# An attention block with a mixture layer on one core: maxima of two PSUM banks in one VectorE operation, a new order of the units, and fewer filler products

## What is computed

```
Xn = layernorm(x) * ln_g + ln_b
Q, K, V = Xn @ Wq + bq, Xn @ Wk + bk, Xn @ Wv + bv      # split in 16 heads
A = softmax(causal(Q K^T / sqrt(16)))
x = layernorm(x + (A V) @ Wo + bo)
```

```
h = relu(x @ W1 + b1);  alpha = softmax(h @ W2 + b2)
x = layernorm(x + sum_k alpha_k * (x @ V_k^T) @ U_k^T)
```

## Time and profile before

| | us |
|---|---|
| median of 3 runs | 436.98 (436.42 to 437.85) |
| profiled execution, its own time | 436.52 |
| its span in the trace | 434.8 |
| TensorE busy | 407.4 (94%) |
| VectorE busy | 309.3 (71%) |
| ScalarE busy | 241.3 (55%) |
| GpSimd busy | 74.6 (17%) |
| mean granted TensorE clock | 0.994 |

### The profile page before, as it was taken

How to read it: one execution, slowest core, us unless ns; L and a number is a source line. 1 busy time by engine, 2 the same in 40 slices (tenths; PEclk the granted TensorE clock), 3 DMA queues, 4 the chain that set the end, 5 groups by cost and what they waited for, 6 DMA issues and landing times.

```text
span 434.8 us, 7330 instructions
## 1 busy us (share of the span) xinstructions
PE 407.4 (94%) x2563; PEld 214.1 (49%) x2563; DVE 309.3 (71%) x805; ACT 241.3 (55%) x535; POOL 74.6 (17%) x111
## 2 busy tenths in 40 slices
PE   7997899999989999999999999999999998998994
PEld 3545444353324445467757844335433444447683
DVE  4638997798798756627478799789879864214665
ACT  5691554766766667542541265567666758552321
POOL 4331210233121010111331021113312011010000
PEclk9999999999998999999999999999999999999999
DMA  6066761450402000000775037145040000000011
GB/s 194 8 100 97 192 96 26 62 85 5 74 1 99 0 3 0 0 2 0 157 132 76 3 77 105 16 67 84 2 75 3 0 3 0 2 0 2 1 48 50
DMA packets 18452, 21.14 MB, mean 49 GB/s; under 512 B 4976, under 2 KB 11888, under 8 KB 18416
## 3 DMA queue, kind: packets, MB, share of 16 engines
q1 hardware_dynamic: 18365, 20.66, 25.5%
q10 hardware_dynamic: 51, 0.01, 0.0%
HBM read 5.79 MB, written 2.10 MB: 18 GB/s over the span
## 4 chain that ended last, share of the span: by engine, by line
PE 71%; DVE 17%; ACT 7%; issue 2%; POOL 1%; DMA 1%; POOLq 0%; DVEq 0%; ACTq 0%
PE ps L881 16%; PE ps L995 14%; PE ps L975 14%; PE ps L952 10%; DVE mx L771 9%; PE ps L889 7%; PE ps L897 2%; PE ps L872 2%; DVE ps L767 2%; ACT pr L641 2%; PE ps L956 2%; PE ps L1005 2%; PE ps L1046 1%; DVE st L704 1%; ACT stk L568 1%
## 5 line engine op out<-in xcount | busy, mean ns | idle before, releaser
L641 ACT ACTIVATE pr<-ps 128x512 f32<-128x512 f32 (+3 forms) x384 | 166.0, 495 | 96.9 <-PE ps L975 95.4
L771 DVE TENSOR_REDUCE mx<-ps 128x1 f32<-128x512 f32 (+3 forms) x240 | 145.7, 666 | 15.1 <-PE ps L952 7.8
L975 PE MATMUL ps<-stq,stk 99*128 99x512 bf16 (+3 forms) x384 | 116.6, 331 | 4.6 <-ACT pr L641 3.3
L952 PE MATMUL ps<-stk,stq 96*128 96x512 bf16 (+3 forms) x384 | 113.2, 328 | 2.1 <-DVE mx L771 0.9
L559 POOL TENSOR_SCALAR_AFFINE_SELECT pr<-pr 128x512 f32<-128x512 f32 x64 | 40.9, 639 | 255.4 <-ACT pr L641 255.4
L995 PE MATMUL ps<-pr,va 128*32 128x512 f32 (+3 forms) x768 | 82.4, 501 | 0.5 <-POOL pr L559 0.5
L975 PEld LDWEIGHTS ps<-stq,stk 99*128 99x128 bf16 x384 | 34.5, 98 | 91.0 <-ACT pr L641 51.8
L952 PEld LDWEIGHTS ps<-stk,stq 96*128 96x128 bf16 x384 | 37.7, 98 | 23.4 <-issue 7.4
L767 DVE CUSTOM_DVE_ANT_0 ps<-ps,causal 128x384 f32<-128x384 f32 (+1 forms) x64 | 38.6, 647 | 11.6 <-PE ps L952 11.6
L956 PE MATMUL ps<-mask,ident_b 128*128 128x128 bf16 x192 | 35.5, 220 | 0.0
L881 PE MATMUL ps<-u_t,avt 128*128 128x256 f32 x128 | 30.7, 382 | 0.2 <-ACT avt L663 0.2
(11 more groups left out here) (95 smaller groups left out, 385.6 us busy)
## 6 DMA issues: line engine op xcount, KB each, us to landing
stq<-qk_raw SPq DMA_DIRECT2D x32, 96.0 KB, 2.8
stk<-qk_raw SPq DMA_DIRECT2D x32, 96.0 KB, 2.8
x_in<-in_x SPq DMA_DIRECT2D x8, 256.0 KB, 3.9
stq<-qk_raw SPq DMA_DIRECT2D x32, 64.0 KB, 2.4
stk<-qk_raw SPq DMA_DIRECT2D x32, 64.0 KB, 2.4
out_y<-x SPq DMA_DIRECT2D x3, 512.0 KB, 3.0
stk<-qk_raw SPq DMA_DIRECT2D x32, 32.0 KB, 2.4
stq<-qk_raw SPq DMA_DIRECT2D x32, 32.0 KB, 2.2
```

Source lines behind the costliest of these rows:

```text
L641: nc.scalar.activation(probs(b, g, s)[:, j, q0 - c * CHUNK:], act_bank(ev)[:, q0 - c * CHUNK:], ACT.Exp, scale=DH ** -0.5).then_inc(s_act_ ...
L771: nc.vector.tensor_reduce(dst, src, AX.X, ALU.max).then_inc(s_dve_free, 1)
L952: last = nc.tensor.matmul(bank[:, i * w:(i + 1) * w], q[0:ROWS, t // TPC, j, tile(t % TPC)], k[0:ROWS, k0 // CHUNK, j, 0:w], start=True, s ...
L975: nc.tensor.matmul(bank[:, q0 - c * CHUNK:], stk[stack_of(b, g)][0:ROWS + PARTS, kt // TPC, j, tile(kt % TPC)], stq[stack_of(b, g)][0:ROWS ...
```

## The change

1. **Pairs.** In g0 and g1, two units of the same tile and keys with heads 0 and 1, or 2 and 3, that stand in adjacent banks are reduced by one `tensor_reduce` over both banks; it frees both banks when it ends. This makes 63 pairs of 126 units. `side_by_side` reorders the units inside a block so that pairs stand in adjacent places of the ring. A pair is not broken by other TensorE work that stands between its two products in the list.
2. **Units dealt anew.** One point of `course` moves a step earlier, so that the units of (g0, c1) are all issued earlier among the scores, and later ones up to three or four places earlier, tapering to none at the end.
3. **Filler.** 13 and 6 products become 5 and 3, in each batch.
4. **Far parts.** The four subtractions go from VectorE to GpSimd.
5. **Opening.** VectorE's wait for the masks goes from the head of its program to the operations that read the mask (once ahead of each of the 64).

```diff
+GROUPS_OF_PAIRS = 2
...
-    course = [(0, needed[0] + 6), (first_step[1], needed[1] + 12), (first_step[2] - 1, needed[2] + 1), (first_step[-1] - 3, needed[-1])]
+    course = [(0, needed[0] + 6), (first_step[1], needed[1] + 12), (first_step[2] - 2, needed[2] + 1), (first_step[-1] - 3, needed[-1])]
...
+def side_by_side(order, units):
...
+    for (b, g, _, _), places in blocks.items():
+        mine = [u for _, _, u in places]
+        pairs = [(u, v) for u, v in zip(mine, mine[1:]) if pair_of(units, u, v)]
+        singles = [u for u in mine if all(u not in pair for pair in pairs)]
...
+    order = with_parts(side_by_side(program_order(NB, G, T, KC), units))
...
+                if kind == "far":
+                    _, _, name, k = ev
+                    whole, split = split_weights[name]
+                    pool.wait_ge(s_weight_near, n_halve["halve", *ev[1:]])
+                    pool.tensor_tensor(split[:, 1, k], whole[:, k], split[:, 0, k].bitcast(F32),
+                                       ALU.subtract).then_inc(s_weight_far, 1)
...
-            dve.wait_ge(s_mask, 6)
...
-                if kind == "far":
...
+                    if ev in second_of:
+                        continue
                     dve.wait_ge(s_dve_full, n_dve[ev])
...
+                    if ev in first_of:
+                        low = (n_dve[first_of[ev]] - 1) % DVE_RING
+                        dst = mx[:, g % 2, t // TPC, k0 // CHUNK, heads[0] - 1:heads[0] + 1, t % TPC]
+                        nc.vector.tensor_reduce(dst, ps[:, low:low + 2, 0:w], AX.X, ALU.max).then_inc(s_dve_free, 2)
+                    elif on_vector(g, units[u]):
+                        dve.wait_ge(s_mask, 6)
...
-                            turn_over(bank, 6 if g else 13)
+                            turn_over(bank, 3 if g else 5)
```

More of the change, by code:

```diff
@@ L30 @@
 RES = 3
+GROUPS_OF_PAIRS = 2
+ON_DVE_RING = ("qk", "fold", "max", "turn", "r1", "lg", "x1t", "vx", "u")
 def max_units(tiles):
@@ L142, in with_parts, with pair_of @@
     return out
+def pair_of(units, u, v):
+    (t, k0, _, heads, _), (t_, k0_, _, heads_, _) = units[u], units[v]
+    return (t, k0) == (t_, k0_) and len(heads) == 1 and heads[0] % 2 == 0 and heads_[0] == heads[0] + 1
+def side_by_side(order, units):
+    order, ring, blocks = list(order), 0, {}
+    for at, ev in enumerate(order):
+        if ev[0] == "max" and ev[2] < GROUPS_OF_PAIRS:
+            half = ev[1:3] == (0, 0) and units[ev[3]][0] < TPC and units[ev[3]][3][-1] < HPG // 2
+            blocks.setdefault((*ev[1:3], units[ev[3]][0] // TPC, not half), []).append((at, ring, ev[3]))
+        ring += ev[0] in ON_DVE_RING
+    for (b, g, _, _), places in blocks.items():
+        mine = [u for _, _, u in places]
+        pairs = [(u, v) for u, v in zip(mine, mine[1:]) if pair_of(units, u, v)]
+        singles = [u for u in mine if all(u not in pair for pair in pairs)]
+        best = {len(places): (0, ()), len(places) + 1: (-1, ())}
+        for i in reversed(range(len(places))):
+            best[i] = best[i + 1]
+            if i + 1 < len(places) and places[i + 1][1] == places[i][1] + 1 and places[i][1] % DVE_RING < DVE_RING - 1:
+                n, rest = best[i + 2]
+                if n + 1 >= best[i][0]:
+                    best[i] = n + 1, (i, *rest)
+        joint = best[0][1][:len(pairs)]
+        whole, broken = pairs[:len(joint)], pairs[len(joint):]
+        singles += [u for pair in broken for u in pair]
+        i = 0
+        while i < len(places):
+            for u in whole.pop(0) if i in joint else (singles.pop(0),):
+                order[places[i][0]] = ("max", b, g, u)
+                i += 1
+    return order
 def woven(*lists):
@@ L375, in block_kernel @@
         n_act = count("xt", "v", "score", "rows", "ot", "h", "avt")
-        n_dve = count("qk", "fold", "max", "turn", "r1", "lg", "x1t", "vx", "u")
+        n_dve = count(*ON_DVE_RING)
+        second_of = {}
+        maxima = [ev for ev in order if ev[0] == "max"]
+        for one, two in zip(maxima, maxima[1:]):
+            if one not in second_of.values() and one[1:3] == two[1:3] and one[2] < GROUPS_OF_PAIRS and pair_of(units, one[3], two[3]):
+                if n_dve[two] == n_dve[one] + 1 and n_dve[one] % DVE_RING:
+                    second_of[one] = two
+        first_of = {two: one for one, two in second_of.items()}
         n_near, n_halve, n_far = count("x1t"), count("halve"), count("far")
@@ L395, in block_kernel @@
         LOADS = 16 * 6
-        first_unit, first_of_half = set(), {}
-        for g in range(G):
-            for c in range(C):
-                mine = block_units(T, g, c)
-                first_unit.add((g, mine[0]))
-                for h in range(2):
-                    u = next(u for u in mine if any(j // 2 == h for j in units[u][3]))
-                    first_of_half.setdefault((g, u), []).append(h)
+        first_unit, first_of_half, seen = set(), {}, set()
+        for ev in order:
+            if ev[0] == "max":
+                block_of = *ev[1:3], units[ev[3]][0] // TPC
+                if block_of not in seen:
+                    first_unit.add(ev)
+                halves = {j // 2 for j in units[ev[3]][3]}
+                first_of_half[ev] = [h for h in sorted(halves) if (*block_of, h) not in seen]
+                seen.update({block_of}, {(*block_of, h) for h in halves})
         def act_bank(ev):
@@ L742, in _ @@
                         part(w, c, 0)[:, m], ALU.add, ALU.subtract).then_inc(s_dve_free, 1)
-                if kind == "far":
-                    _, _, name, k = ev
-                    whole, split = split_weights[name]
-                    dve.wait_ge(s_weight_near, n_halve["halve", *ev[1:]])
-                    nc.vector.tensor_tensor(split[:, 1, k], whole[:, k], split[:, 0, k].bitcast(F32),
-                                            ALU.subtract).then_inc(s_weight_far, 1)
                 if kind == "x1t":
@@ L760, in _ @@
                     t, k0, w, heads, _ = units[u]
+                    if ev in second_of:
+                        continue
                     dve.wait_ge(s_dve_full, n_dve[ev])
-                    if (g, u) in first_unit and b * G + g >= 2:
+                    if first_of.get(ev, ev) in first_unit and b * G + g >= 2:
                         dve.wait_ge(s_split, n_split["split", *divmod(b * G + g - 2, G), t // TPC])
                     dst = mx[:, g % 2, t // TPC, k0 // CHUNK, heads[0]:heads[-1] + 1, t % TPC]
-                    if on_vector(g, units[u]):
+                    if ev in first_of:
[4 more added lines that the diff above has]
+                        dve.wait_ge(s_mask, 6)
                         nc.vector.tensor_tensor_reduce(dve_bank(ev)[:, 0:w], dve_bank(ev)[:, 0:w], causal[:, CHUNK - w:], 1.0, -FLT_MAX,
@@ L945, in _ @@
                     q, k = stq[stack_of(b, g)], stk[stack_of(b, g)]
-                    for h in first_of_half.get((g, u), []):
+                    for h in first_of_half[ev]:
                         pe.wait_ge(s_stack[stack_of(b, g)][t // TPC][h], LOADS * ((b * G + g) // STACKS + 1))
```

1 line of the change is left out of this document (removed).

## The result

The changed kernel takes 440.17 us (median of 20 runs, 439.08 to 441.05) against 437.87 for the kernel before, measured beside it (20 runs, 434.72 to 441.26). The ratio is 1.0058, with a 95% interval of 1.0036 to 1.0081: slower by some 0.6%. The forecast was 432.0. The profiled execution took 439.58, with a span of 437.6 (before: 436.52 and 434.8).

The account below looks back on a forecast made before the run. VectorE was taken to bound the units of (g0, c1), TensorE other stretches. Terms -1.0, -3.3, -0.1 and -0.6 sum to -5.0 from 436.52: 431.5, as a median 432.0; own range 429.5 to 434.5, full range 428.0 to 435.5.

Parts of the forecast that it names:

- Opening: Start of the kernel: VectorE no longer idles for GpSimd's mask, so the first transposes start earlier; -1.0 us.
- Far parts: Four subtractions moved to GpSimd, hidden between its selections, giving batch 0 the pace of batch 1; -3.3 us.
- both halves of the term: Batch 0: -1.65 us of VectorE time ahead of the split of (g2, c1), and -1.65 from the clock after its wait.
- pace of pairs: VectorE's paired reductions were to start 1.13 us apart.
- the price of the pairs: Idle VectorE in (g0, c1), 1.2 per batch against 0.8 saved, plus 0.9 and 0.4 us in earlier blocks.
- Stretches that TensorE sets, where a faster VectorE is worth nothing: Stretches of a batch outside those VectorE sets; a removed product was to be worth its full time there.
- Units anew and filler: New deal and fewer filler products: +0.7 and +0.5 at (g0, c1), -0.65 per batch ahead of (g1, c1).
- the wait at (g2, c1): TensorE's wait for VectorE at this rows product was to shrink with units dealt earlier; -0.3 each batch, -0.6 us.
- The trip of 3.89 us from product to score: Ahead of (g0, c1)'s first score: the trip was to stay the same, so 8 filler products less gain nothing by themselves.
- three units done earlier: Three units more done by the first score of (g0, c1), a gain of 0.5 us.
- The fall at 130 us: Clock at 0.50 after batch 0's 1.96 us wait at (g2, c1); was to go with the shorter wait, -1.65 us.
- The rival on the clock: New waits from pairs and less filler, at two or more places, make the clock fall; 441 us, chance 0.07.

Follow-up runs that it names:

- far_tail: The kernel before with the four far subtractions on GpSimd and nine filler products in the waits at the end of the second batch; 433.36 us, ratio 0.990.
- order_only: The changed kernel with its unit order kept but every unit reduced by itself, each bank given back at once; 433.30 us, ratio 0.989.
- Late_start: The changed kernel with single reductions, where a pair's first unit waits until the second's bank is full, each bank freed at once; 437.23 us.
- late_release: The changed kernel with single reductions starting when their bank is full, but both banks of a pair given back only after the second; 434.17 us.
- late_both: The changed kernel with single reductions under both restrictions: first waits for the second's bank, both banks given back by the second; 440.88 us.
- open_far_less_filler: The kernel before with the mask wait moved, far parts on GpSimd, and 5 and 3 filler products; old deal, order and reductions; 432.30 us.
- no_pairs: The changed kernel with no pairs and no reordering of units inside a block; new deal, less filler, far parts and moved wait kept; 433.15 us.
- the first four: The first four follow-up kernels, which asked which edit loses the time; the kernel before, timed beside them, took 436.63 us.
- least_filler: The kernel before with mask wait moved, far parts on GpSimd, 5 and 1 filler products, and nine more at the second batch's end; 429.33 us.
- open_far_only: The kernel before with only the mask wait moved and the four far subtractions on GpSimd; 433.93 us, ratio 0.989.

## Why the prediction was wrong, step by step

**Right.** *Opening*: first transposes at 8.59 (forecast 8.7), first weight products 1.3 us earlier (forecast 1.0). That it came so close is luck: in the 15 profiles with the moved wait the first weight products start at 10.20 to 11.77, in the three without it at 11.84 or 11.85. *Far parts*: 3.3 us by far_tail's D, the sum of both halves of the term; GpSimd hid its work. The *pace of pairs*, 1.14 us.

**The step that failed is the price of the pairs.** The prediction put it at 2.1 us, or 2.4 with its rounding in batch 1. The runs show 7.0. Set against order_only by the rows products, the changed kernel lost:

| | forecast | measured |
|---|---|---|
| ahead of (g1, c0)'s rows product, batch 0 and 1 | 0.9 and 0.4 | 1.66 and 0.79 |
| (g0, c1) | 0.4 and 0.4 | 1.14 and 1.71 |
| (g1, c1), up to the rows product of (g2, c1) | 0 and 0 | 0.79 and 0.93 |

The 1.66 are the difference of 1.15 and 0.51 by which the changed kernel's first weight products started earlier in its profile (10.54 against 11.05). Two things were missed:

- *The mechanism was half of it.* The text priced the late release, "frees both at its end, so TensorE has 1.13 us", and the idle VectorE where a value product splits a pair. Late_start and late_release show the late start as the larger part, and late_both that the two feed each other: a bank that waits full for its neighbour is also given back later, and the neighbour's product then comes later still. In (g0, c1) the price was 1.2 idle less 0.8 saved. From the end of the split of (g1, c0) to its last maximum the block takes VectorE 16.54 us in batch 0 and 16.84 in batch 1, against 15.74 in both in order_only: 0.80 and 1.10 lost. The rows product then comes another 0.34 and 0.61 later behind that maximum. Batch 1 was put at "mostly by less" for its five split pairs and lost more than batch 0.
- *(g1, c1) was not priced.* "Stretches that TensorE sets, where a faster VectorE is worth nothing" is true of the gain and was taken over for the cost. There a wait for a bank is TensorE's own time, and 12 pairs of each batch lie there.

**Units anew and filler** was put at -3.1 (the -0.1 and the -0.6 for the wait at (g2, c1), less 2.4 for the pairs). The filler was worth 3.1 by D: ahead of (g1, c1) the 0.65 per batch of the forecast, ahead of (g0, c1) 0.9 where the forecast had nothing. "The trip of 3.89 us from product to score" was no trip but filler: with 5 products in place of 13 it is 67.92 - 64.94 = 2.98, and TensorE waits for the rows in it. The wait at (g2, c1) did not shrink (0.79 in open_far_less_filler, 0.82 in no_pairs), so the -0.6 was worth nothing. The new deal took 2.1 of the gain back: no_pairs has D 280.08 against 278.02 in open_far_less_filler, and they differ in the deal alone. The spans show 1.95 of it, the medians 0.85. The three units done earlier are thus no gain. Nearly all of it lies between the rows transfers of (g1, c1) and (g2, c1), 1.0 in each batch, not at (g0, c1), where the new order is easiest to see; why the deal costs this was not tried.

**The clock.** The fall at 130 us went, as the prediction said, and one came at 396 us. The rival on the clock was right in kind (a fall in a new place) and wrong in its cause: the place has the same waits in both kernels, and the fall came there when the one at 130 us was gone. Its 441 lies near the measured time by luck: it counted on waits of 2 us at the split of (g1, c0) and at the rows of (g0, c1), and these are 1.11 and none. So 1.7 us of the far gain is seen in the attention and given back at the end, until the end is filled too.

The ledger, by spans: opening and far -2.7, filler -2.9, deal and order +2.2, pairs +7.0; together +3.7 from 434.5 (the kernel before beside the first four), which gives 438.2. (By medians it is -2.7, -1.6, +1.0 and +6.9, from 436.6 to 440.2.) Forecast were -4.3, -3.1 for filler, deal and the wait together, and +2.4. The 3.7 are more than the 2.3 between the first two medians, 440.17 and 437.87, since the runs of the kernel before spread with the clock, from 434.7 to 441.3: at a mean clock of 0.994 to 0.995 it took 436.1 to 437.6 beside the experiments, the changed kernel 439.1 to 441.1.

The Trainium skill (VectorE: DVE Perf Modes, the table of op costs) gave 120 cycles, an estimate of 0.125 us a pair. A single reduction's own duration has 0.683 - 0.533 = 0.150 beside its columns, near the page; in a row only 0.06 of it is there to save, as forecast.

## What to carry to other kernels

An operation over two banks of a ring waits for the later and holds the earlier, and both hurt whichever engine leads: price both in stretches where the consumer leads and in those where the producer does. Join only what is produced back to back; the reordering cost nothing, and the 16 adjacent pairs were free and worth nothing either. Measure filler against the landing of what it covers, and put some of it where the waits at the end of the kernel are: open_far_less_filler with nine such products (tail_filler), 429.6 us, is 2.1% faster than the kernel before and the best here beside least_filler's 429.3.

## What was not expected of the hardware

All 18 profiles end at a granted clock of 0.50. Ahead of that, 14 have one or two stretches at 0.50, and they lie in different places: near 43, near 130, at 388 to 396 or at 406 to 410 us in most. A fall costs 1.7 us: of the kernel before, the runs beside the experiments with a mean clock of 0.997 to 0.998 took 434.7 to 435.5 us, those at 0.994 to 0.995 436.1 to 437.6, those at 0.984 440.4 to 441.3. The Trainium skill (TensorE: Matmul & The Clock Gate, The HAM clock gate) has activity keep the fast clock. The runs agree, with a price: nine products of 0.22 us in three waits gave 1.5, 2.0 and 0.9 us of span in three kernels. They also show what one trace cannot: a fall that an edit removes may only have moved.

The opening varies too. The 20 filler products last 0.61 to 0.63 us each at first and 0.38 later (kernel before, up to 5 and from 7 us; the profile's clock reads 1.00 all along). They took 5.78 us in open_far_only's profile and 6.75 in that of open_far_less_filler, and the transposes behind them, with their inputs ready, started at 8.24 and 9.21. With VectorE's wait gone, it is this filler that sets the opening, and one profile does not measure it.
